# Full-array tiles and unread constant products in the block inversions of two attention stages

## The chip, the cores and the metric

The kernel runs on one core of one Trainium2 chip. The metric is the device time of the whole launch in microseconds, the median of several executions; lower is better. Everything is float32, except for five mask tables that are bfloat16.

## The reference, cut to what matters

The launch computes one network of four layers, each an attention block and a feed-forward block, on 8 batches of 512 rows of 128 columns. The change concerns two of the eight blocks: the first layer's attention (stage L0) and the third layer's (stage L2). Both are delta rules with 4 heads of 32 key columns. L0's reference has the step that matters, a triangular inverse of each chunk:

```python
A = jnp.where(tri, 0.0, -jnp.einsum('bhncd,bhned->bhnce', kb, k))
for i in range(1, chunk):
    upd = jnp.einsum('...k,...kj->...j', A[..., i, :], A[..., :, :i])
    A = A.at[..., i, :i].add(upd)
inv = A + jnp.eye(chunk, dtype=A.dtype)
u, w = inv @ v, inv @ kb
# per chunk, in order:
u_adj = ui - wi @ S
out_i = qi @ S + attn @ u_adj
S = S + jnp.swapaxes(ki, -1, -2) @ u_adj
```

L2 is the gated form of the same recurrence, stepwise in the reference. The kernel computes both in chunks of 128 rows: one 128x128 inverse for each chunk and head.

## The kernel before, in words

**Stages and lanes.** Eight stages run one after the other (`program`). Within a stage a unit is one batch of 512 rows (4 tiles). Two lanes work on two units at once; `weave` alternates their phases one by one, and every engine gets its instructions in that order. A lane has four PSUM banks `b[0..3]`. L0 and L2 have 8 units each, so 4 rounds of two units. A unit has four chunks, taken as two pairs.

**One pair of one unit**, in phases (`delta_phases`). The score products (L782) give the matrix `NT` and the masked attention `AT`. ScalarE copies `NT` out of PSUM in L0 (L1179); VectorE does in L2 (L2882). ScalarE then copies the four diagonal 32x32 blocks of `NT` into the tile `strict` (L856), laid out as 64x64 tiles with zeros beside the blocks. VectorE makes level 0 out of it: an add of the two halves, a mask product, a subtraction, a transposition (L885, 887, 889, 891).

**Levels 1 to 4** (`levels_pe`). Each has a left and a right phase. Left (L801): for each of the 8 matrices `m` two products of a 64x64 tile of `strict` with 32 columns of `x`. VectorE masks the result (L899). Right (L809): 32 products of 32x32 tiles with 16 columns. VectorE subtracts (L906) and transposes (L909), which gives the next `x`. The profile has two records for each float32 product, so a left phase is 32 records of L801 and a right phase 64 of L809.

**The joins**: `left_5`, `right_5`, `turn`, `left_6`, `right_6` (L817, 826, 834, 841, 848) put the 32-blocks together to 64 and then to 128, on tiles of 32x32 and 64x64.

**The chunks**: `carry`, `u`, `out`, one after the other over the chunks, on 128x128 tiles: in L0 L1089 and L1090, then L935, L1099 and L1101; in L2 L2663, L935, L2671 and L2675. Each carries the state `S` on.

**What else is in these stretches.** In L0 the first pair of every round has the products of the 64-tap filter between its phases: `next(between, None)` issues six products (12 records of L1243, 128x64 tiles with 16 columns) behind each phase. L2 has for each pair two products of `after` with 512 columns (L2651) ahead of the scores.

**Stage ends.** `meet_all` makes PE, ScalarE, VectorE and GpSimd wait on every semaphore that has a count, those of the DMAs too. `program` issues the load of the next stage's weights at the start of a stage; the stage function calls `meet_all` again after its first few instructions, so this wait includes the load just issued. `weights_landed` has a wait of its own on the current stage's weights.

**`held`** is one product and one ScalarE copy with bias (L1174) of L0, which stands among the key copies; PE waits for it ahead of the first scores.

Of the kernel before, what the change touches and what calls it, by code (L numbers as in the profile page):

```python
# [149 lines left out]

class Run:
# [22 lines left out]
    def meet(self, engine):  # L174

        for s in self.steps.values():
            if s.count:
                engine.wait_ge(s.sem, s.count)
# [240 lines left out]
def turn(pe, u, c, bank, blocks, name, rows=P):  # L419

    for t, block in enumerate(blocks):
        done = pe.transpose(bank[0:rows, t * P:(t + 1) * P], block, c("ident"))  # L422
    done.then_inc(*u.pe.step(name))

# [326 lines left out]

class Delta:
# [5 lines left out]
    def __init__(self, c, arena, dv, scaled):  # L758
# [6 lines left out]
        self.strict = arena.take(INVERTED, 2 * SMALL)  # L765
        self.strict_half = [self.strict[:, :, n * SMALL:(n + 1) * SMALL] for n in range(2)]
# [21 lines left out]
    def start_dve(self, dve, u):  # L788

        dve.memset(self.XT, 0.0).then_inc(*u.dve.step())  # L790
        dve.memset(self.strict, 0.0).then_inc(*u.dve.step("strict_cleared"))

    def levels_pe(self, pe, u, pair, between):
        b = u.banks
        for n in range(1, SMALL_LEVELS):
            pe.wait_ge(*u.dve.at(f"x{pair}_{n - 1}"))
            if n == 1:
                pe.wait_ge(*u.act.at(f"strict{pair}"))
            for m in range(INVERTED):
                for g in map(half_of, range(2)):  # L800
                    made = pe.matmul(b[2][g, m * SMALL:(m + 1) * SMALL], self.strict[g, m, :], self.x[g, m, :])  # L801
            made.then_inc(*u.pe.step(f"left{pair}_{n}"))
            next(between, None)
            yield f"left{pair}_{n}"
            pe.wait_ge(*u.dve.at(f"part{pair}_{n}"))
            half = SMALL // 2
            for m in range(INVERTED):
                for q in map(quarter, range(QUARTERS)):
                    made = pe.matmul(packed(b[3][q, m * half:(m + 1) * half], n), self.part[q, m, :],  # L809
                                     odd_blocks(self.xt[q, m, :], n))  # L810
            made.then_inc(*u.pe.step(f"right{pair}_{n}"))
            next(between, None)
            yield f"right{pair}_{n}"
# [6 lines left out]
        next(between, None)  # L820
        yield f"left{pair}_5"
# [7 lines left out]
        next(between, None)  # L829
        yield f"right{pair}_5"  # L830
# [12 lines left out]
        next(between, None)  # L843
        yield f"left{pair}_6"
# [8 lines left out]
    def strict_act(self, act, u, pair):  # L853

        for i in range(QUARTERS):
            act.copy(self.strict_half[i % 2][quarter(i)], self.NT8[quarter(i), :, quarter(i)]).then_inc(*u.act.step(f"strict{pair}"))  # L856
# [26 lines left out]
    def level0_dve(self, dve, u, pair):  # L883
        dve.wait_ge(*u.act.at(f"strict{pair}"))
        dve.tensor_tensor(self.part, *self.strict_half, ALU.add).then_inc(*u.dve.step())  # L885
        dve.wait_ge(*u.dve.last())
# [90 lines left out]
class L0AttnLane:  # L977
    def __init__(self, c, arena, vT, shortT, vearly, vrow):
# [3 lines left out]
        self.before = {name: arena.take(L0_ATTN_CONV - 1 + SEQ) for name in "qkv"}  # L982
        self.stat_rows = arena.take(TILES, HEADS, 32)
# [16 lines left out]
class L0Attn:  # L1000
    def __init__(self, run, w, arena, X):
# [7 lines left out]
                      for lane in range(LANES)]  # L1009
        self.units, self.filters, self.products = units_of(run, ["l0_attn"]), None, None  # L1010
# [29 lines left out]
    def pe(self, pe, u):  # L1040
        m, b, w, c = self.lanes[u.lane], u.banks, self.w, self.c
# [26 lines left out]
        turn(pe, u, c, b[2], tiles_of(m.qrow), "qT")  # L1068
        yield "keys"
# [3 lines left out]
        for pair in range(CHUNKS // 2):  # L1073
            if pair == 0:
                pe.wait_ge(*u.act.at("keyed"))
                pe.wait_ge(*u.act.at("held"))
            else:
                pe.wait_ge(*u.act.at("got1"))
                pe.wait_ge(*u.dve.at("state1"))
            yield from d.score_pe(pe, u, pair, m.kT, m.kbq)  # L1080
            yield from d.levels_pe(pe, u, pair, products)
            for j in range(2):
# [20 lines left out]
                made.then_inc(*u.pe.step(f"out{chunk}"))  # L1103
                yield f"out{chunk}"
# [33 lines left out]
    def act(self, act, u):  # L1138
# [27 lines left out]
        act.activation(m.rn, m.ss, ACT.Sqrt).then_inc(*u.act.step("norms"))  # L1166
        yield "norms"
# [5 lines left out]
        act.wait_ge(*u.pe.at("held"))  # L1173
        act.activation(m.zT, b[3][:, :], ACT.Identity, bias=w("fuse_b1")).then_inc(*u.act.step("held"))  # L1174
# [243 lines left out]
    def pool(self, pool, u):  # L1418
# [5 lines left out]
        for pair in range(CHUNKS // 2):  # L1424
            yield from delta_phases(pair)
# [1133 lines left out]
class L2AttnLane:  # L2559
    def __init__(self, c, arena):  # L2560
# [7 lines left out]
        self.conv = [all_heads(v) for v in (self.gt[:, 0], self.gt[:, 1], self.gtm[:, 0], self.gtm[:, 1])]  # L2568
        self.steps = [self.a, self.delta.T1[:, 0]]
# [10 lines left out]
class L2Attn:  # L2580
    def __init__(self, run, w, arena, X):
        self.run, self.c, self.w, self.X = run, run.c, w, X
        self.rate = arena.take(HEADS)
        self.lanes = [L2AttnLane(run.c, arena) for _ in range(LANES)]

# [11 lines left out]
    def pe(self, pe, u):  # L2597
        m, b, w, c = self.lanes[u.lane], u.banks, self.w, self.c
# [47 lines left out]
        for pair in range(CHUNKS // 2):  # L2646
            if pair > 0:
                pe.wait_ge(*u.dve.at("got1"))
            for j in range(2):
                pe.wait_ge(*u.dve.at(f"steps{pair}_{j}"))  # L2650
                pe.matmul(b[2 + j][:, :], c("after"), flat(m.steps[j])).then_inc(*u.pe.step(f"between{pair}_{j}"))  # L2651
            yield f"between{pair}"
# [3 lines left out]
            for j in range(2):  # L2656
# [19 lines left out]
                made.then_inc(*u.pe.step(f"out{chunk}"))  # L2676
                yield f"out{chunk}"
# [263 lines left out]
    def pool(self, pool, u):  # L2941
# [11 lines left out]
        for pair in range(CHUNKS // 2):  # L2953
            yield f"between{pair}"
            yield from delta_phases(pair)
# [918 lines left out]
```

## Time and profile before

| | |
|---|---|
| time, median of 3 runs | 5654.37 us (5648.27 to 5659.23) |
| the profiled execution's own time | 5665.99 us |
| its span, first to last instruction | 5664.6 us |
| PE busy in the span | 4062.2 us (72%) |
| VectorE, ScalarE, GpSimd busy | 3020.7, 1912.0, 818.4 us |
| mean granted TensorE clock | 0.76 of full speed |

The granted clock is the share of TensorE's full 2.4 GHz; it has two levels in this profile, 0.50 (1.2 GHz) and 1.00. A mean between them is a stretch with both. L0 runs from the start to about 1000 us, L2 from about 2844 to 3814 us.

### The profile page before, as it was taken

The numbers are of one execution on the slowest core, as the hardware profiler recorded it, in microseconds if no ns is written. First come the engines' busy times: TensorE is split into PE (matmuls) and PEld (weight loads), VectorE is DVE, ScalarE is ACT, GpSimd is POOL, SyncE is SP. The second block draws the span as 40 slices with busy tenths as digits, with TensorE's granted clock in tenths as the row PEclk, the third lists the DMA queues.
The fourth block names the chain that finished last, engine by engine and source line by source line (L and its number), as shares of the span: only waits on it lengthen the run. The fifth ranks groups of instructions, "written<-read, shape, count | busy, mean of one in ns | idle before, by whom it ended". The sixth has DMA issues, their size and how long they took to land.

```text
span 5664.6 us, 93833 instructions
## 1 busy us (share of the span) xinstructions
PE 4062.2 (72%) x39179; PEld 3146.2 (56%) x39228; DVE 3020.7 (53%) x8021; ACT 1912.0 (34%) x4196; POOL 818.4 (14%) x600
## 2 busy tenths in 40 slices
PE   6685967568878778773757768577777777776398
PEld 5574846446556555562646557464444555445377
DVE  4445364234554555547255665657666666665333
ACT  2234232123333333330232332325444455552122
POOL 0000000321011101101700000001222111110444
PEclk6555555677898898885756666668888998897599
DMA  9200000330000000001210000000000000000255
GB/s 266 54 2 1 2 1 1 105 113 1 1 1 1 1 1 1 1 1 37 31 41 1 1 1 2 1 2 1 1 1 1 1 1 1 1 1 17 72 164 141
DMA packets 140856, 152.26 MB, mean 27 GB/s; under 512 B 7809, under 2 KB 128003, under 8 KB 139793
## 3 DMA queue, kind: packets, MB, share of 16 engines
q1 hardware_dynamic: 119024, 128.21, 7.7%
q0 software_dynamic: 21408, 18.05, 1.9%
q8 instruction: 309, 5.06, 0.4%
q14 instruction: 115, 0.93, 0.1%
HBM read 87.38 MB, written 59.76 MB: 26 GB/s over the span
## 4 chain that ended last, share of the span: by engine, by line
PE 50%; DVE 29%; ACT 13%; issue 3%; POOL 3%; DMA 2%; SPq 0%; DVEq 0%; POOLq 0%; ACTq 0%
ACT work L3242 4%; PE banks_lane L801 4%; PE banks_lane L422 3%; PE banks_lane L3679 2%; PE banks_lane L1882 2%; PE banks_lane L809 2%; PE banks_lane L3128 2%; PE banks_lane L935 2%; PE banks_lane L3163 1%; ACT work L1976 1%; PE banks_lane L3108 1%; PE banks_lane L3150 1%; POOL room_l_ffn L569 1%; DVE work L2797 1%; DVE weights L3252 1%
## 5 line engine op out<-in xcount | busy, mean ns | idle before, releaser
L422 PE MATMUL banks_lane<-constants,work 128*128 128x128 f32 x968 | 194.4, 346 | 456.2 <-DVE work L408 209.2
L422 PEld LDWEIGHTS banks_lane<-constants,work 128*128 128x128 f32 x968 | 145.3, 178 | 524.9 <-DVE work L408 196.9
L422 PE MATMUL banks_lane<-constants,weights 128*128 128x128 f32 x596 | 126.2, 349 | 349.8 <-DVE weights L408 94.9
L402 POOL TENSOR_TENSOR weights<-weights,constants 128x4 f32<-128x4 f32 x76 | 78.6, 1034 | 1929.6 <-DVE weights L397 1929.6
L422 PEld LDWEIGHTS banks_lane<-constants,weights 128*128 128x128 f32 x596 | 89.3, 180 | 381.6 <-issue 175.0
L3242 ACT ACTIVATE work<-banks_lane,weights 128x192 f32<-128x192 f32 (+1 forms) x512 | 249.3, 505 | 132.5 <-DVE weights L3339 132.5
L402 POOL TENSOR_TENSOR work<-work,constants 128x4 f32<-128x4 f32 x76 | 77.5, 1019 | 1208.8 <-DVE work L397 1208.8
L3346 POOL TENSOR_TENSOR weights<-weights,constants 128x16 f32<-128x16 f32 x64 | 185.5, 2898 | 377.3 <-DVE weights L3254 377.3
L3335 DVE TENSOR_REDUCE weights<-banks_lane 128x2 f32<-128x384 f32 (+1 forms) x256 | 122.4, 520 | 140.2 <-PE banks_lane L3150 140.2
L2029 DVE TENSOR_REDUCE work<-banks_lane 128x2 f32<-128x512 f32 x256 | 158.8, 683 | 67.7 <-PE banks_lane L1896 67.2
L3163 PE MATMUL banks_lane<-constants,work 128*128 128x128 f32 x896 | 135.5, 297 | 80.7 <-DVE work L3327 42.2
L1976 ACT ACTIVATE work<-banks_lane 128x384 f32<-128x384 f32 (+1 forms) x256 | 118.5, 549 | 178.2 <-PE banks_lane L1917 110.0
L3163 PEld LDWEIGHTS banks_lane<-constants,work 128*128 128x128 f32 x896 | 108.1, 152 | 104.5 <-issue 57.0
L3679 PE MATMUL banks_lane<-weights,work 128*128 128x256 f32 x624 | 145.1, 386 | 14.5 <-DVE weights L3721 14.5
L3178 PE MATMUL banks_lane<-work 128*64 128x128 f32 x1792 | 128.1, 288 | 37.2 <-ACT work L3204 37.2
L656 POOL DMA_INDIRECT out<-weights,chunk_places x78 | 121.5, 1558 | 196.5 <-DVE chunk_places L648 130.3
L569 POOL DMA_INDIRECT room_l_ffn<-weights,indices x96 | 92.8, 966 | 362.1 <-DVE weights L392 324.7
L1882 PE MATMUL banks_lane<-weights,work 128*128 128x128 f32 x1024 | 136.7, 298 | 5.9 <-ACT work L1998 5.9
L1882 PEld LDWEIGHTS banks_lane<-weights,work 128*128 128x128 f32 x1024 | 132.7, 213 | 10.3 <-ACT work L1998 10.3
L801 PE MATMUL banks_lane<-work 64*64 64x32 f32 x2048 | 125.1, 292 | 16.5 <-DVE work L891 13.0
L3679 PEld LDWEIGHTS banks_lane<-weights,work 128*128 128x128 f32 x624 | 116.9, 192 | 34.0 <-DVE weights L3721 19.3
L3178 PEld LDWEIGHTS banks_lane<-work 128*64 128x64 f32 x1792 | 100.7, 142 | 62.2 <-ACT work L3204 49.6
(773 smaller groups left out, 10869.7 us busy)
## 6 DMA issues: line engine op xcount, KB each, us to landing
work<-experts_dram_l_ffn SPq DMA_DIRECT2D x39, 964.0 KB, 4.9
room_l_ffn<-work SPq DMA_DIRECT2D x30, 1188.0 KB, 14.7
work<-experts_dram_l_ffn SPq DMA_DIRECT2D x23, 512.0 KB, 3.6
weights<-weights_dram SPq DMA_DIRECT2D x1, 4833.5 KB, 14.3
work<-room_l_ffn SPq DMA_DIRECT2D x36, 132.0 KB, 4.0
weights<-weights_dram SPq DMA_DIRECT2D x1, 4112.0 KB, 13.1
weights<-bands_dram SPq DMA_DIRECT2D x1, 4096.0 KB, 13.1
weights<-room_l_ffn SPq DMA_DIRECT2D x26, 132.0 KB, 4.3
```

The source lines that it names most:

```text
L402: pool.tensor_tensor(n.rstd, n.rstd, c("neghalf", cols=(0, n.rstd.shape[1])), ALU.pow).then_inc(*u.pool.step(name))
L422: done = pe.transpose(bank[0:rows, t * P:(t + 1) * P], block, c("ident"))
L569: pool.indirect_dma_start(self.room, bass.IndirectOffsetOnAxis(ap=self.where[:, n, t:t + 1], axis=0), rows[n][:, t, :], None).then_inc(*se ...
L801: made = pe.matmul(b[2][g, m * SMALL:(m + 1) * SMALL], self.strict[g, m, :], self.x[g, m, :])
L1882: made = pe.matmul(b[1][:, cols_of(t)], m.ff[:, f, cols_of(t)], self.w(u, f"down{f}"), start=f == 0, stop=f == L1_ATTN_FF - 1)
L1976: act.activation(m.probs[:, hh, 0:blocks, :].rearrange("p b q -> p (b q)"), b[hh][:, 0:blocks * P], ACT.Exp, scale=L1_ATTN_SCALE).then_inc ...
L2029: dve.tensor_reduce(m.top[r][:, :, hh, L1_ATTN_HD], b[hh][:, :].rearrange("p (t c) -> p t c", t=2), AX, ALU.max, negate=True).then_inc(*u. ...
L3163: made = pe.transpose(u.banks[2 + side][:, cols_of(hh)], m.probs[n % 2][:, hh, side * P:(side + 1) * P], self.c("ident"))
L3178: made = pe.matmul(u.banks[2][rows, cols_of(j)], m.v[:, t - 1 + side, at:at + L2_FFN_HD], m.turned[n % 2][:, 4 * side + hh, :], start=side ...
L3242: act.activation(m.probs[n % 2][:, hh, L2_FFN_BACK + lo:2 * P], u.banks[side][:, j * span:(j + 1) * span], ACT.Exp, scale=m.q_factor[:, t, ...
L3346: pool.tensor_tensor(m.rn[:, t, :, :], m.rn[:, t, :, :], c("neghalf", cols=(0, 2 * L2_FFN_HEADS)).rearrange("p (n h) -> p n h", n=2), ALU. ...
L3679: made = pe.matmul(bank[:, g * CHUNK:(g + 1) * CHUNK], self.w(u, f"{name}{f}", cols=(g * P, (g + 1) * P)), m.z[:, f, :], start=f == 0, sto ...
```

## The change

The left phase takes `strict` as block-diagonal 128x128 tiles: 8 products of a 128x128 tile with 32 columns in the place of 16 of 64x64. The tiles are made by GpSimd, two products of `NT` with the constant `blocks32` for each pair (`blocks_pool`), written into buffers that are free then. ScalarE's four copies go into `part` directly, and VectorE's add of the halves and one memset go away. `keep_busy` issues products of two constant bfloat16 masks, a 128x128 tile with 512 columns, into a bank that nobody reads: one behind each half level and behind three of the join phases; in L0 2 (lane 0) or 8 (lane 1) behind the key transpositions; one behind a pair's first chunk, four behind the first pair's second chunk; in L2 four before and four behind the two products of each pair ahead of its scores. `held` moves ahead on ScalarE. `meet` leaves out the semaphores of the weights. In the cut diff below, the `keep_busy` line shown behind `left{pair}_{n}` also stands behind `right{pair}_{n}` and, with `FILL_JOIN`, behind `left{pair}_5`, `right{pair}_5` and `left{pair}_6`; L2's GpSimd program has the same two lines as L0's, with a wait on VectorE's `nt{pair}`. Fills by count: 264 in L0 (176 in levels and joins, 40 behind keys, 48 behind chunks) and 352 in L2 (176, 48, and 128 around the products ahead of the scores).

```diff
+WEIGHTS = [("DMA", f"weights{n}") for n in range(2)]
...
     def meet(self, engine):
-        for s in self.steps.values():
-            if s.count:
+        for key, s in self.steps.items():
+            if s.count and key not in WEIGHTS:
                 engine.wait_ge(s.sem, s.count)
...
+def keep_busy(pe, masks, place, n):
+
+    for _ in range(n):
+        pe.matmul(place, masks("ident"), masks("later"), start=True, stop=True)
...
+FILL_LEVEL, FILL_JOIN, FILL_CHUNK, FILL_PAIR, FILL_BETWEEN = 1, 1, 1, 4, 4
+FILL_KEYS = [2, 8]
...
-        self.strict = arena.take(INVERTED, 2 * SMALL)
-        self.strict_half = [self.strict[:, :, n * SMALL:(n + 1) * SMALL] for n in range(2)]
+        self.strict = None
...
         dve.memset(self.XT, 0.0).then_inc(*u.dve.step())
-        dve.memset(self.strict, 0.0).then_inc(*u.dve.step("strict_cleared"))
...
             if n == 1:
-                pe.wait_ge(*u.act.at(f"strict{pair}"))
+                pe.wait_ge(*u.pool.at(f"blocks{pair}"))
             for m in range(INVERTED):
-                for g in map(half_of, range(2)):
-                    made = pe.matmul(b[2][g, m * SMALL:(m + 1) * SMALL], self.strict[g, m, :], self.x[g, m, :])
+                made = pe.matmul(b[2][:, m * SMALL:(m + 1) * SMALL], self.strict[m // HEADS][:, m % HEADS, :], self.x[:, m, :])
             made.then_inc(*u.pe.step(f"left{pair}_{n}"))
             next(between, None)
+            keep_busy(pe, self.masks, b[0][:, :], FILL_LEVEL)
             yield f"left{pair}_{n}"
...
     def strict_act(self, act, u, pair):
         for i in range(QUARTERS):
-            act.copy(self.strict_half[i % 2][quarter(i)], self.NT8[quarter(i), :, quarter(i)]).then_inc(*u.act.step(f"strict{pair}"))
+            act.copy(self.part[quarter(i)], self.NT8[quarter(i), :, quarter(i)]).then_inc(*u.act.step(f"strict{pair}"))
+
+    def blocks_pool(self, pool, u, pair):
+
+        blocks = per_tile(self.c("blocks32"), HEADS)
+        for chunk in range(2):
+            pool.tensor_tensor(self.strict[chunk], self.NT[:, chunk], blocks, ALU.mult).then_inc(*u.pool.step(f"blocks{pair}"))
...
         dve.wait_ge(*u.act.at(f"strict{pair}"))
-        dve.tensor_tensor(self.part, *self.strict_half, ALU.add).then_inc(*u.dve.step())
-        dve.wait_ge(*u.dve.last())
         dve.tensor_tensor(self.part, self.part, per_tile(self.c("small0"), INVERTED), ALU.mult).then_inc(*u.dve.step())
...
         turn(pe, u, c, b[2], tiles_of(m.qrow), "qT")
+        pe.wait_ge(*u.act.at("held"))
+        keep_busy(pe, masks, b[3][:, :], FILL_KEYS[u.lane])
         yield "keys"
...
                 pe.wait_ge(*u.act.at("keyed"))
-                pe.wait_ge(*u.act.at("held"))
...
                 made.then_inc(*u.pe.step(f"out{chunk}"))
+                if chunk < CHUNKS - 1:
+                    keep_busy(pe, masks, b[0][:, :], FILL_PAIR if j else FILL_CHUNK)
                 yield f"out{chunk}"
@@ L0Attn.act, before yield "norms" @@
+        act.wait_ge(*u.pe.at("held"))
+        act.activation(m.zT, b[3][:, :], ACT.Identity, bias=w("fuse_b1")).then_inc(*u.act.step("held"))
@@ and before yield "keys" @@
-        act.wait_ge(*u.pe.at("held"))
-        act.activation(m.zT, b[3][:, :], ACT.Identity, bias=w("fuse_b1")).then_inc(*u.act.step("held"))
@@ L0Attn.pool @@
         for pair in range(CHUNKS // 2):
+            pool.wait_ge(*u.act.at(f"nt{pair}_{HEADS - 1}"))
+            m.delta.blocks_pool(pool, u, pair)
             yield from delta_phases(pair)
@@ L2Attn.pe @@
+            keep_busy(pe, masks, b[0][:, :], FILL_BETWEEN)
             for j in range(2):
                 pe.wait_ge(*u.dve.at(f"steps{pair}_{j}"))
                 pe.matmul(b[2 + j][:, :], c("after"), flat(m.steps[j])).then_inc(*u.pe.step(f"between{pair}_{j}"))
+            keep_busy(pe, masks, b[0][:, :], FILL_BETWEEN)
             yield f"between{pair}"
...
                 made.then_inc(*u.pe.step(f"out{chunk}"))
+                if chunk < CHUNKS - 1:
+                    keep_busy(pe, masks, b[1][:, :], FILL_PAIR if j else FILL_CHUNK)
```

## Rows read from the trace of the kernel before

**Rows 1.** The page: granted clock in 40 slices, in tenths.

```profile
PEclk6555555677898898885756666668888998897599
```

**Rows 2.** Windows: busy us of PE, PEld, DVE, ACT, POOL; clock; DMA.

```profile
318.00:331.00 13.00, 7.42 (x166) 5.40 (x164) 9.07 (x22) 9.06 (x23) 0.00 (x0) 1.00 0.01 2
340.00:349.00 9.00, 9.00 (x250) 8.65 (x248) 2.60 (x8) 0.00 (x0) 0.00 (x0) 0.50 0.01 4
377.00:396.00 19.00, 19.00 (x98) 18.54 (x96) 4.97 (x15) 2.19 (x7) 0.00 (x0) 0.50 0.00 1
2980.00:2987.00 7.00, 7.00 (x34) 6.34 (x32) 3.09 (x7) 0.37 (x1) 0.00 (x0) 0.50 0.00 0
2988.00:3000.00 12.00, 11.13 (x77) 9.00 (x76) 8.15 (x17) 2.31 (x5) 0.00 (x0) 1.00 0.00 0
```

**Rows 3.** The chain in L0, a first pair: start us, us, what.

```profile
340.44 1.85 PE banks_lane L801 x32
342.29 0.76 PE banks_lane L1243 x12
...
345.66 0.98 PE banks_lane L809 x64
...
349.14 1.85 PE banks_lane L801 x32
```

**Rows 4.** The chain in L0, second pair, the same columns.

```profile
408.62 3.63 PE banks_lane L801 x64
...
414.12 3.72 PE banks_lane L801 x63
```

**Rows 5.** Timeline of PE in L0 at clock 1.00: start, us, what.

```profile
325.67 1.17 PE L782 MATMUL banks_lane<-work 32*128 32x256 f32 x16 [2.50 <-ACT work L1174]
326.78 1.12 PE L801 MATMUL banks_lane<-weights,work 64*64 64x32 f32 x32
327.83 0.53 PE L1243 MATMUL banks_lane<-weights 128*64 128x16 f32 x12
329.68 0.73 PE L809 MATMUL banks_lane<-weights,work 32*32 32x16 f32 x64 [1.33 <-DVE work L899]
```

**Rows 6.** Timeline of PE, chunks of L0, then of L2.

```profile
380.36 1.91 PE L935 MATMUL banks_lane<-work,weights 128*128 128x32 f32 x8
...
385.07 1.90 PE L935 MATMUL banks_lane<-work 128*128 128x32 f32 x8
...
2987.17 1.10 PE L935 MATMUL banks_lane<-work 128*128 128x64 f32 x8
...
2990.44 1.10 PE L935 MATMUL banks_lane<-weights 128*128 128x64 f32 x8
```

**Rows 7.** Timeline of PE in L1: four bfloat16 mask products.

```profile
1341.19 1.10 PE L1891 MATMUL banks_lane<-masks 128*128 128x512 bf16 x4 [1.15 <-ACT work L1965]
```

**Rows 8.** The chain of the whole span: loads of weights.

```profile
1209.37 14.31 DMA weights<-weights_dram
...
2844.43 10.37 DMA weights<-weights_dram
```

**Rows 9.** Timeline: VectorE beside a GpSimd product, and alone.

```profile
1226.40 1.26 POOL L2080 TENSOR_TENSOR work<-work,weights 128x512 f32<-128x512 f32 x1
1226.47 2.05 DVE L408 TENSOR_SCALAR work<-work 128x128 f32<-128x128 f32 x4 [1.21 <-POOL work L402]
...
2857.63 1.12 DVE L408 TENSOR_SCALAR weights<-x_rows,weights 128x128 f32<-128x128 f32 x4 [1.25 <-POOL weights L402]
```

**Rows 10.** Timeline in L0: the copies and level 0 of one unit.

```profile
399.62 1.68 ACT L856 COPY work<-weights 32x256 f32<-32x256 f32 x4
...
401.34 0.42 DVE L885 TENSOR_TENSOR work<-work 128x256 f32<-128x256 f32 x1 [0.60 <-ACT work L856]
```

**Rows 11.** Timeline of PE in L2, ahead of a second pair's scores.

```profile
3003.73 3.18 PE L2651 MATMUL banks_lane<-work,constants 128*128 128x512 f32 x4 [3.83 <-DVE work L2873]
3007.60 2.11 PE L782 MATMUL banks_lane<-work 32*128 32x256 f32 x16 [0.69 <-ACT work L2760]
```

More of the change, by code:

```diff
@@ L812, in levels_pe @@
             next(between, None)
+            keep_busy(pe, self.masks, b[0][:, :], FILL_LEVEL)
             yield f"right{pair}_{n}"
@@ L820, in levels_pe @@
         next(between, None)
+        keep_busy(pe, self.masks, b[0][:, :], FILL_JOIN)
         yield f"left{pair}_5"
@@ L829, in levels_pe @@
         next(between, None)
+        keep_busy(pe, self.masks, b[0][:, :], FILL_JOIN)
         yield f"right{pair}_5"
@@ L843, in levels_pe @@
         next(between, None)
+        keep_busy(pe, self.masks, b[0][:, :], FILL_JOIN)
         yield f"left{pair}_6"
@@ L982, in __init__ @@
         self.before = {name: arena.take(L0_ATTN_CONV - 1 + SEQ) for name in "qkv"}
+        self.delta.strict = [self.before[name][:, L0_ATTN_CONV - 1:].rearrange("p (h n) -> p h n", n=P) for name in "qk"]
         self.stat_rows = arena.take(TILES, HEADS, 32)
@@ L1009, in __init__ @@
                       for lane in range(LANES)]
+        for m in self.lanes:
+            m.delta.masks = run.masks
         self.units, self.filters, self.products = units_of(run, ["l0_attn"]), None, None
@@ L1040, in pe @@
     def pe(self, pe, u):
-        m, b, w, c = self.lanes[u.lane], u.banks, self.w, self.c
+        m, b, w, c, masks = self.lanes[u.lane], u.banks, self.w, self.c, self.run.masks
         d = m.delta
@@ L2568, in __init__ @@
         self.conv = [all_heads(v) for v in (self.gt[:, 0], self.gt[:, 1], self.gtm[:, 0], self.gtm[:, 1])]
+        self.delta.strict = [self.gt[:, 0], self.gt[:, 1]]
         self.steps = [self.a, self.delta.T1[:, 0]]
@@ L2584, in __init__ @@
         self.lanes = [L2AttnLane(run.c, arena) for _ in range(LANES)]
+        for m in self.lanes:
+            m.delta.masks = run.masks
     def start_act(self, act, u):
@@ L2597, in pe @@
     def pe(self, pe, u):
-        m, b, w, c = self.lanes[u.lane], u.banks, self.w, self.c
+        m, b, w, c, masks = self.lanes[u.lane], u.banks, self.w, self.c, self.run.masks
         d = m.delta
@@ L2954, in pool @@
             yield f"between{pair}"
+            pool.wait_ge(*u.dve.at(f"nt{pair}"))
+            m.delta.blocks_pool(pool, u, pair)
             yield from delta_phases(pair)
```

## Prediction

> **What bounds the kernel now.** I read the page's slices first. PE is busy 72% of the span, but the clock row shows that this is often not work at full speed: the first slices (L0, 0 to 1000 us) and the middle ones (L2, from 2844 us) stand at 5 to 7 tenths, the stages between at 8 and 9 [rows 1]. Then the windows inside those two stages. In a first pair of L0, from 340 to 349 us, PE is busy 9.00 of 9.00 us at clock 0.50, 1.2 GHz; in the chunks from 377 to 396 us it is busy throughout, on 128x128 tiles, and still at 0.50. In L2 the clock goes from 0.50 to 1.00 at about 2987 us, behind some 7 us of full tiles with 64 and 256 columns, and stays up while such tiles go on [rows 2]. So being busy is not what raised it; streaming many columns through the full array is what the stretches with the high clock share, and the levels' small tiles and few columns are what those with the low clock share.
>
> Third, the chain. In the levels it runs on PE alone, piece behind piece: left phase 1.85 us, filter products 0.76, right phase 0.98, for two lanes; from one lane's left phase to its next is 349.14 - 340.44 = 8.70 us [rows 3], without filter products 414.12 - 408.62 = 5.50 us [rows 4]. VectorE and ScalarE are hidden behind the other lane. What PE issues, and at which clock, is therefore time one to one. There are 8 units by 2 pairs in each stage, two lanes at a time: 16 stretches in all, of 4 levels each, of which 4 (the first pairs of L0) have filter products.
>
> Last, the chain holds 14.31 and 10.37 us of waiting for weights [rows 8].
>
> **The change part by part, against the span of the profiled execution, if the clock holds in the levels.**
>
> *Left phase.* 16 records of a full tile with 32 columns take the place of 32 of 64x64. At half clock L935, the same shape, takes 1.91 us for 8 records [rows 6], so 16 take 3.5 to 3.8 (the tail of the first group lies under the second); I take 3.5, against 1.85 now. At full clock the trace has 64 columns, 1.10 us for 8 [rows 6]: 1.8 to 2.2 for 16, I take 1.9. So the new tile only breaks even at the double clock, and it costs 1.65 us more for each lane and level if the clock does not come.
>
> *Fills.* Four mask products of 512 columns take 1.10 us [rows 7], so one is 0.24 (without the shared tail) to 0.28; I take 0.24, and 0.48 at half clock. 616 of them are 148 us at full clock, 296 at half. In the levels nothing hides them, since PE is the chain. Ahead of the scores PE idles 3.83 us for VectorE in L2 [rows 11] and 2.50 us in L0 [rows 5]; the fills there cost nothing at full clock (8 are 1.9 us).
>
> *The rest of a level* at full clock: a right phase is 0.73 us with its tail, a group of filter products 0.53 [rows 5]; I take 0.55 and 0.40 from start to start. A level of both lanes is then 2 x (1.9 + 0.24 + 0.55 + 0.24) = 5.9 us, against 5.50: +0.4, over 12 stretches of 4 levels +17 us. With filter products 5.9 + 4 x 0.40 = 7.5, against 8.70: -1.2, over 16 levels -20 us. The levels themselves thus give nothing back; what is gained is what they let stay fast.
>
> *Joins.* Three fills for each lane, 1.4 us of both lanes at full clock and 2.9 at half, against small tiles that are halved where the clock is up; they are short chains through ScalarE. From -4 to +3 a stretch; I take -1: -16 us.
>
> *Chunks.* In L0 a step of one lane is 385.07 - 380.36 = 4.71 us at half clock; in L2 at full clock 2990.44 - 2987.17 = 3.27 [rows 6]. With a fill, three of four steps gain 1.2 us: 8 stretches, -29 us. L2's clock comes 7 us into its chunks [rows 2]; if it comes sooner, 0 to -3.5 us a stretch, I take -1.5: -12 us.
>
> *Scores of second pairs, and L2651.* A score phase is 2.11 us [rows 11], 1.17 at full clock [rows 5]. Two lanes in 4 stretches of L0: -8. In L2 about -2 for each of 8 stretches, L2651's 3.18 [rows 11] being nearly halved but waited for: -16. Together -24 us.
>
> *Held.* PE waits for it ahead of the second lane's scores [rows 5]; moved, it saves up to its 0.7 us four times: -3. Behind it on ScalarE stand the key copies, which wait for PE's transpositions anyway.
>
> *GpSimd.* Two products of 1.26 us [rows 9] stand where ScalarE's copies, 1.68 [rows 10], were what the first left phase waited for; VectorE loses one 0.42 us step of level 0 [rows 10]. GpSimd has nothing else queued in these phases. But beside a GpSimd product four VectorE instructions took 2.05 us that take 1.12 alone [rows 9], so level 0, with inputs from SBUF, may wait until GpSimd is done: 0.84 later, 0.42 shorter. At 0.4 us over 32 unit pairs +13 at most on the chain, half of it under the other lane; I take +8. The bounds are -13 (VectorE's step gained, nothing blocked) and 64 x 0.93 = +60.
>
> The Trainium skill, "SBUF — State Buffer", "Who interferes with whom", says that a VectorE instruction with two SBUF inputs and a GpSimd instruction reading SBUF block each other for a whole instruction. The trace agrees in kind, with 0.93 us lost beside one of 1.26; by the rule alone the bound would be 64 x 1.26 = 81 us in the place of 60.
>
> *Weights.* The two loads leave the chain and have a stage to land in: -24.7 us, sure.
>
> Sum: +17 - 20 - 16 - 29 - 12 - 24 - 3 + 8 - 25 = -104 us. The profiled execution's own time is 5666, so 5562; it lay 12 us above the median of the runs, so 5550.
>
> **The rivals.**
>
> *The clock falls in the levels (slower).* This is decided in one place. The new level has full tiles of 32 columns for 3.8 of 5.9 us, as the chunks of L0 that stayed at 0.50 have [rows 2], and fills of 512 columns for 1.0 us, which those lack. If fills and tiles are not enough, it falls behind the first level at full clock and nothing in the levels raises it again. A level is then 2 x (3.5 + 0.48 + 0.98 + 0.48) = 10.9 us against 5.50, with filter products 13.9 against 8.70: 5.3 more, for 3 levels of 16 stretches +254; joins +46; the chunks keep two thirds of their gain, -29; scores -20; the rest -20. Sum +231: 5885. It turns from gain to loss where about 20 of the 64 levels are at half clock. For it: the levels' average is not far from stretches that were slow. Against it: the clock is at 1.00 from 318 to 331 us, with PE busy only 7.42 of 13 us [rows 2], on full-tile transpositions, scores and one product of 512 columns: wide work with long gaps is enough. The fills also stand evenly, one behind each half level, and the filter products and joins are the only parts with less.
>
> *It falls in some stretches*, for instance in those with filter products, which dilute the fills: half way, +64: 5718.
>
> *GpSimd becomes what level 1 waits for, and blocks VectorE*, at the bound of +60 with the clock held: -52: 5602. For it rows 9; against it that only level 0 meets these products.
>
> *The Trainium skill*, "TensorE: Matmul & The Clock Gate", "Why this matters for your kernels", has it that keeping TensorE busy without long idle gaps gives the full clock. By that rule the clock would hold here, as in the forecast, but it would also have been up in the levels before, where 9.00 of 9.00 us busy stood at 0.50. The trace does not agree; I give the rule no more than the forecast has.
>
> **How the numbers follow.** Clock holds 0.58 (own range 5460 to 5610: joins and chunks wholly gained, or levels at the upper bounds of tile and fill); GpSimd blocks 0.07; falls in some stretches 0.14; falls in the levels 0.21. Same means within 0.2%, 11 us, about what a measurement of this kernel can tell from no change. Faster: 0.57 + 0.07 + 0.05 of the partial case = 0.69; same 0.04; slower 0.27. The range for 8 in 10 runs from 5440, below which only more gain than every part's bound would lead, to 5780, which takes in the partial case and leaves most of the last.
>
> **What would show it.** Right: windows in the levels of L0 and L2 at clock 0.9 to 1.0; left phases of about 1.9 us from start to start; 5.9 and 7.5 us a level; no piece of weights in the chain; chunk steps near 3.4 us in L0. Wrong: levels of 10 us or more at 0.50; idle time of PE ahead of the first left phase that GpSimd ends; level-0 instructions of VectorE of over 1 us; fills that delay the scores of the second lane.

## The result and the profile after

The changed kernel takes 5968.61 us (median of 4 runs, 5963.41 to 5985.8) against 5653.37 us before: ratio 1.0563, 95% interval 1.0539 to 1.0587. The recorded forecast was 5550 us, so it missed the sign. What came is the rival in which the clock falls in the levels, at +315 us by the medians and +297.5 by the spans (5962.1 and 5664.6), where the rival had +231 on the span. The ratio of fills2_entry4 below leaves out its slowest run, 5906.54 us, which is 1.8% above its fastest; its median is of all four.

The page of after, its first lines and the clock in 40 slices:

```profile
PE 4425.8 (74%) x37796; PEld 3367.0 (56%) x37796; DVE 3035.0 (51%) x7985; ACT 1913.2 (32%) x4196; POOL 900.0 (15%) x664
...
PEclk6555555577799888885766666666888898988599
```

PE has 364 us more to do and its clock is no higher: L0 is at 5 tenths from its second slice on, L2 at 6. Compare the clock row of before [rows 1]. Next, the windows (columns as in [rows 2]) in a first pair of L0, then in a first pair of L2:

```profile
361.00:366.00 5.00, 4.19 (x107) 3.47 (x106) 4.52 (x9) 2.84 (x8) 2.94 (x2) 1.00 0.01 3
366.00:380.00 14.00, 13.50 (x212) 12.19 (x213) 8.33 (x13) 0.00 (x0) 0.00 (x0) 0.52 0.01 2
380.00:412.00 32.00, 32.00 (x454) 28.77 (x453) 5.07 (x13) 0.81 (x2) 0.00 (x0) 0.50 0.01 2
...
3084.00:3089.00 5.00, 3.76 (x94) 2.79 (x86) 4.70 (x12) 1.61 (x4) 2.50 (x2) 1.00 0.00 0
3089.00:3093.00 4.00, 3.11 (x17) 3.12 (x18) 1.42 (x4) 0.00 (x0) 0.00 (x0) 0.69 0.02 4
3093.00:3110.00 17.00, 17.00 (x312) 14.78 (x312) 3.90 (x10) 0.00 (x0) 0.00 (x0) 0.50 0.01 2
```

The clock is 1.00 when level 1 starts, falls within it, and from there PE is busy without a gap at 0.50. In 15 of the 16 stretches it fell within level 1 (in three second pairs of L0 it had come up only in the first half us of it); in L0's first second pair, at 178.0 us, it stood at 0.50 throughout. Levels 2 to 4 are at 0.50 in all 16. The Trainium skill, "TensorE: Matmul & The Clock Gate", "Why this matters for your kernels", has it that an engine kept busy gets the full clock; 32.00 of 32.00 us busy at 0.50 is against it here, as [rows 2] were.

The timeline of PE in L0's first pair shows the fall and what a level costs behind it (start, us, line; in brackets idle time and its releaser; L811 is the left phase, L1268 the filter products, L432 the unread products, L820 the right phase):

```profile
360.94 1.97 PE L811 MATMUL banks_lane<-weights,work 128*128 128x32 f32 x16
362.84 0.53 PE L1268 MATMUL banks_lane<-weights 128*64 128x16 f32 x12
363.30 0.39 PE L432 MATMUL banks_lane<-masks 128*128 128x512 bf16 x1
364.48 0.73 PE L820 MATMUL banks_lane<-weights,work 32*32 32x16 f32 x64 [0.80 <-DVE work L918]
...
366.50 3.49 PE L811 MATMUL banks_lane<-work 128*128 128x32 f32 x16 [0.51 <-DVE work L910]
...
371.08 3.46 PE L811 MATMUL banks_lane<-weights,work 128*128 128x32 f32 x16
...
380.19 3.46 PE L811 MATMUL banks_lane<-work 128*128 128x32 f32 x16
```

From one lane's left phase to its next, 380.19 - 366.50 = 13.69 us, against 8.70 before [rows 3]; the rival had 13.9. The same in L2, without filter products:

```profile
3084.53 1.97 PE L811 MATMUL banks_lane<-weights,work 128*128 128x32 f32 x16
...
3087.87 0.73 PE L820 MATMUL banks_lane<-weights 32*32 32x16 f32 x64 [1.16 <-DVE weights L918]
...
3089.89 3.09 PE L811 MATMUL banks_lane<-work 128*128 128x32 f32 x16 [0.97 <-DVE work L910]
...
3093.20 3.46 PE L811 MATMUL banks_lane<-weights,work 128*128 128x32 f32 x16
...
3099.92 3.46 PE L811 MATMUL banks_lane<-work 128*128 128x32 f32 x16
...
3103.60 0.69 PE L811 MATMUL banks_lane<-weights,work 128*128 128x32 f32 x3
```

The other lane's left phases stand at 3093.20 and 3103.60: 10.40 us a level, against 5.50 before [rows 4]; the rival had 10.9. At half clock an unread product takes 0.40 us from its start to the next one's where a left phase follows and 0.54 where small tiles do. In these two the lane that comes first has its left phase of level 1 at clock 1.00, 1.97 us, about the 1.9 of the forecast; the other's takes 3.49 and 3.09.

Summed over the 16 stretches by the timelines of the two kernels (level 1's first left phase to `left_5`; `left_5` to the first L935, L954 in after; that to the last of the pair):

| us | levels | joins | chunks |
|---|---|---|---|
| before | 426 | 270 | 235 |
| after | 688 | 320 | 232 |

+262, +50 and -3 make +309; all else together gives back 12.

VectorE's timeline at the entry (L906 is level 0's mask product), and GpSimd's at the same time:

```profile
358.22 1.10 DVE L906 TENSOR_TENSOR work<-work,constants 128x256 f32<-128x256 f32 x1 [0.92 <-ACT work L871]
359.36 0.42 DVE L908 TENSOR_TENSOR weights<-constants,work 128x256 f32<-128x256 f32 x1
...
364.35 1.15 DVE L906 TENSOR_TENSOR work<-work,constants 128x256 f32<-128x256 f32 x1
```

```profile
356.55 2.50 POOL L877 TENSOR_TENSOR work<-weights,constants 128x512 f32<-128x512 f32 x2 [38.47 <-ACT weights L1204]
362.28 2.94 POOL L877 TENSOR_TENSOR work<-work,constants 128x512 f32<-128x512 f32 x2 [3.23 <-ACT work L1204]
```

Beside GpSimd's products L906 takes 1.10 and 1.15 us; L908, of the same size, 0.42 behind them, and each step of level 0 took 0.42 before [rows 10]. The add of 0.42 that went away is paid for with 0.7 on the step behind it. The Trainium skill, "SBUF — State Buffer", "Who interferes with whom", says that a VectorE instruction with two SBUF inputs and a GpSimd one that reads SBUF block each other; the trace agrees in kind, with 1.10 and 1.15 us in the place of 0.42.

### The profile page after: what moved, and what is told of

Same layout as the page of the kernel before. It is cut to its first block and busy times, and to the rows that moved or that the text cites. A ratio compares the mean times of both kernels' runs of the same rounds, so it can differ in the third digit from the quotient of the medians.

```text
span 5962.1 us, 91016 instructions
## 1 busy us (share of the span) xinstructions
PE 4425.8 (74%) x37796; PEld 3367.0 (56%) x37796; DVE 3035.0 (51%) x7985; ACT 1913.2 (32%) x4196; POOL 900.0 (15%) x664
## 5 line engine op out<-in xcount | busy, mean ns | idle before, releaser
L432 PE MATMUL banks_lane<-masks 128*128 128x512 bf16 x616 | 297.8, 533 | 3.5 <-ACT work L2787 3.5
L811 PEld LDWEIGHTS banks_lane<-work 128*128 128x128 f32 x1024 | 227.9, 328 | 21.8 <-DVE work L910 17.4
L811 PE MATMUL banks_lane<-work 128*128 128x32 f32 x1024 | 221.7, 392 | 12.1 <-DVE work L910 12.1
L811 PEld LDWEIGHTS banks_lane<-weights,work 128*128 128x128 f32 x1024 | 206.5, 300 | 13.8 <-DVE weights L910 5.5
L811 PE MATMUL banks_lane<-weights,work 128*128 128x32 f32 x1024 | 199.8, 366 | 2.6 <-DVE weights L910 2.6
L877 POOL TENSOR_TENSOR work<-weights,constants 128x512 f32<-128x512 f32 x32 | 40.0, 1272 | 1057.7 <-DVE weights L2916 535.4
L886 ACT COPY weights<-weights 32x256 f32<-32x256 f32 x32 | 12.9, 404 | 573.2 <-DVE weights L925 572.8
L918 DVE TENSOR_TENSOR work<-banks_lane,constants 128x256 f32<-128x256 f32 x96 | 40.8, 425 | 276.1 <-PE banks_lane L811 276.1
```

Of the source, the lines that this page charges most:

```text
L432: pe.matmul(place, masks("ident"), masks("later"), start=True, stop=True)
L811: made = pe.matmul(b[2][:, m * SMALL:(m + 1) * SMALL], self.strict[m // HEADS][:, m % HEADS, :], self.x[:, m, :])
```

## The experiments

Eleven kernels ran. Each ratio is against runs of the kernel before on the same chip; a difference of two ratios is turned into us with 5660. By their intervals such a difference is good to 25 to 40 us among the kernels with four runs and to about 10 among those with ten or more. "Fills" are the unread products of L432.

**1. no_level_fills**: the changed kernel, no fills in levels and joins.

```diff
-FILL_LEVEL, FILL_JOIN, FILL_CHUNK, FILL_PAIR, FILL_BETWEEN = 1, 1, 1, 4, 4
+FILL_LEVEL, FILL_JOIN, FILL_CHUNK, FILL_PAIR, FILL_BETWEEN = 0, 0, 1, 4, 4
```

> The changed kernel without the 352 fills in the levels and joins; tiles and all other fills as changed. Theory (the clock falls in level 1 and the fills are lost time at half clock): at half clock a fill adds 0.40 us behind a left phase and 0.54 behind small tiles, nothing hides them; some 300 of 352 stand at half clock: 352 x 0.45 = about -158 us, to 5810 +- 25, and the clock in levels 2 to 4 stays at 0.50. Rival (the fills do keep part of the levels at full clock and pay for themselves): 5968 or more.

5875.91 us, ratio 1.0359 (1.0327 to 1.0391): 0.0204 or 115 us under the changed kernel. The clock is at 0.50 in levels 2 to 4 here too. Levels 611, joins 268, chunks 249: the levels and joins are 129 us shorter, the chunks 17 longer, since L2's stand at 0.77 to 0.82 where six of the changed kernel's eight are at 1.00. A level at 0.50 is 8.9 us by PE's timeline in L2:

```profile
3048.94 3.62 PE L811 MATMUL banks_lane<-work 128*128 128x32 f32 x16
3052.37 3.60 PE L811 MATMUL banks_lane<-weights,work 128*128 128x32 f32 x16
3055.90 1.05 PE L820 MATMUL banks_lane<-work 32*32 32x16 f32 x64
...
3057.84 3.62 PE L811 MATMUL banks_lane<-work 128*128 128x32 f32 x16
```

3057.84 - 3048.94 = 8.90, so the four fills of a level add 10.4 - 8.9 = 1.5 us, not the 2 x 0.40 + 2 x 0.54 = 1.9 that they take themselves: with a fill behind it a left phase is 3.27 us from start to start (3096.47 - 3093.20 in the changed kernel's timeline), without one 3.43 and 3.53. That and the chunks are why 115 us went and not the 158 expected; the fills in levels and joins are still a third of the loss.

**2. old_tiles**: the changed kernel with the 64x64 tiles by ScalarE and VectorE's add, fills as in the change.

```diff
-                made = pe.matmul(b[2][:, m * SMALL:(m + 1) * SMALL], self.strict[m // HEADS][:, m % HEADS, :], self.x[:, m, :])
+                for g in map(half_of, range(2)):
+                    made = pe.matmul(b[2][g, m * SMALL:(m + 1) * SMALL], self.strict[g, m, :], self.x[g, m, :])
...
```

> The changed kernel with the left product on 64x64 tiles again, made by ScalarE as before; all fills stay. Theory: the tile costs 3.4 - 1.85 = 1.55 us for each lane and level at half clock, 128 of them, less where the clock was up, so -180 us, plus a little for the level-1 wait that GpSimd made: 5780 +- 25. The clock in the levels is 0.50 either way. Rival (the tiles carry what clock there is, and without them it is worse): above 5850.

5824.23 us, ratio 1.0261 (1.0225 to 1.0297): 0.0302 or 171 us under the changed kernel, for tile and GpSimd together. Levels 537, so 151 us shorter, joins and chunks as in the changed kernel; a level at 0.50 is 7.8 us (10.9 with filter products) in the place of 10.4 (13.7). Without GpSimd and without the full tile the clock fell in level 1 too, in 13 stretches, and in three second pairs of L0 it stood at 0.50 before; so neither is needed for the fall.

**3. entry4**: the changed kernel with four fills in level 1, one after it.

```diff
-            keep_busy(pe, self.masks, b[0][:, :], FILL_LEVEL)
+            keep_busy(pe, self.masks, b[0][:, :], 4 if n == 1 else FILL_LEVEL)
... (the same behind right)
```

> The changed kernel with 4 fills instead of 1 behind both halves of level 1 only. It asks where the clock is lost. Entry theory (level 1 has idle PE, 0.5 to 1.4 us at a time, behind VectorE's late level 0; once past it one fill a half level would hold): levels 2 to 4 at clock 1.00 in most stretches, a level 6 us instead of 10: more than 200 us faster than the change, below 5770. Fill theory (one fill a half level is too little anywhere): the clock falls in level 2, a few us later than now; 6 more fills for each of 32 lane stretches at 0.22 to 0.43 us: 5968 + 20 to 70, 5990 to 6040.

5915.67 us, ratio 1.0437 (1.04 to 1.0475): 71 us under the changed kernel and between the two forecasts. The timeline of PE in L2 (3055 us) shows the gaps shortened and the clock kept:

```profile
3057.87 0.73 PE L820 MATMUL banks_lane<-weights 32*32 32x16 f32 x64 [0.25 <-DVE weights L918]
...
3059.89 1.97 PE L811 MATMUL banks_lane<-work 128*128 128x32 f32 x16 [0.32 <-DVE work L910]
...
3067.08 1.87 PE L811 MATMUL banks_lane<-work 128*128 128x32 f32 x16
```

At 1.00 the levels behind level 1 take 6.4 and 5.8 us; 5.9 was forecast. In 12 of the 16 stretches the clock was kept through level 1; in four it fell there still, with idle times of 0.3 to 0.7 us. Only 5 of 16 stretches were still at 1.00 in level 3, and none came to the joins with it (joins 321, as in the changed kernel). The four first pairs of L0, with filter products, all fell in level 2, at a mean clock of 0.65 to 0.67 there, and took 13.7 us a level from then on. So what happens in level 1 decides whether the clock outlives it in most stretches, and one fill a half level does not keep it after that. Whether the idle time there or the little that is issued does it, this run does not separate, since the fills change both.

**4. fills3**: the changed kernel with FILL_LEVEL = 3.

> The changed kernel with 3 fills instead of 1 behind every half level. If three are enough, levels run at clock 1.00 and take 2 x (1.8 + 0.65 + 0.55 + 0.65) = 7.3 us instead of 10.1 (13.7 with filter products): about -130 us to -170 with what follows, 5800 to 5840, still slower than before the change. If they are not enough, 4 more fills of 0.43 us for each of 64 levels of two lanes ... 8 x 0.43 x 64 = +220: 6190.

5879.92 us, but from 5813.12 to 5957.23 in four runs; ratio 1.0365 (1.0298 to 1.0433). Windows of two stretches of the same code in one execution:

```profile
3342.00:3371.00 29.00, 28.00 (x617) 21.75 (x617) 12.12 (x31) 2.42 (x6) 2.50 (x2) 1.00 0.01 3
3514.00:3556.00 42.00, 40.80 (x621) 30.67 (x617) 12.67 (x32) 2.42 (x6) 2.50 (x2) 0.67 0.01 2
```

The same 617 products of four levels take 29 us where the clock stays and 42 where it falls in level 1 and comes back in level 3. It came back within the levels in 10 of the 16 stretches; in the changed kernel it never did. Two windows of another stretch, before and after the clock comes back in its level 3:

```profile
3007.00:3035.00 28.00, 27.57 (x345) 20.11 (x345) 6.83 (x16) 0.30 (x1) 1.17 (x1) 0.51 0.01 2
3035.00:3045.00 10.00, 10.00 (x251) 8.05 (x251) 3.05 (x8) 0.81 (x2) 0.00 (x0) 0.99 0.02 4
```

A level at 1.00 is 7.5 us, 9.6 with filter products: more than before at 0.50 (5.50 and 8.70).

**5. weights_only**: the kernel before, where `meet` leaves out the weights.

```diff
+WEIGHTS = [("DMA", f"weights{n}") for n in range(2)]
...
-        for s in self.steps.values():
-            if s.count:
+        for key, s in self.steps.items():
+            if s.count and key not in WEIGHTS:
```

> The kernel before with the weights' semaphores left out of meet, and nothing else. The two pieces of the chain, 14.31 and 10.37 us, go: -24.7 us, ratio 0.9956, if the load of the next weights disturbs nothing. Rival: the load that is now beside the stage's first work slows it, or something else stands at the same place, such as GpSimd or the rows' own load: -10 us or less.

5669.74 against 5676.41 us, ratio 0.9989 (0.9973 to 1.0004): 6 us where 24.7 were forecast. The chain at the start of L2 in this kernel:

```profile
2841.47 7.03 DMA x_rows<-spread
```

and VectorE's timeline at the start of L1 in the kernel before:

```profile
1216.80 0.91 DVE L1803 MEMSET work<- 128x1024 f32 x1 [0.28 <-DVE work L408]
...
1223.77 0.87 DVE L392 BATCH_NORM_STATS2 work<-work 128x6 f32<-128x128 f32 x4 [1.92 <-DMA weights<-weights_dram]
```

The wait for weights on the path was 1.92 us, not 14.31: under the load VectorE did two units' statistics and two sets of memsets that it has to do anyway. In L2, from x landed to the first statistics, it was 2854.88 - 2844.16 = 10.7 us before and 2852.67 - 2848.50 = 4.2 us here, 6.5 saved. The piece of the chain [rows 8] named what came last, not what it cost.

**6. old_tiles_bare**: as old_tiles, and no fills in levels and joins. Left of the change: weights, `held`, and 264 fills at keys, ahead of scores and in chunks.

> The changed kernel with the 64x64 tiles of before and no fills in levels and joins; what is left of the change is the weights' wait, held's place, and the 264 fills at keys, between, chunks and pair ends. Theory that all of the loss is the tile and the level and join fills: weights -25, held -3, the remaining fills about level (a chunk's fill costs 0.25 us a step in L0, the fills ahead of L2's scores stand in idle time, the clock comes a little sooner in L2's chunks): 5615 to 5640, faster than before. Rival, that the remaining fills are a loss of their own (264 x 0.25 to 0.43 = +66 to +110): 5690 or more.

5687.26 against 5676.41 us, ratio 1.0012 (0.9998 to 1.0025). Levels 426 and joins 272 are those of before; chunks 247 against 235. The fills in the chunks cost time, and the clock of the chunks is no higher: 0.50 in all of L0's, 0.76 to 0.84 in L2's, as before.

**7. fills2_entry4**: FILL_LEVEL = 2 with four in level 1.

> The changed kernel with 4 fills behind the half levels of level 1 and 2 behind the others. With 3 the clock held in some stretches and was lost in level 1 in others; with 4 in level 1 it was never lost there. If 2 are enough behind it: clock 1.00 in all 16 stretches, a level 6.4 us (8.0 with filter products), levels 460 us in sum instead of 688, joins and chunks as in the stretches of fills3 that stayed up: 5590 to 5620, faster than before, which would be the time of my forecast's kind. If 2 are not enough with filter products or in part of the stretches: 5700 to 5850.

5853.32 us (5802 to 5907), ratio 1.0278 (1.0231 to 1.0326). In L2 level 3 is at 1.00 in all 8 stretches, 6.7 us a level, and five kept the clock to the end. Three of L0's first pairs fell in level 2 and one in level 3 (15.4 us a level from then on), and of its second pairs three were at 0.50 when level 1 started and one fell in it. So four fills in level 1 do not always keep the clock there, as entry4's trace had shown. A held stretch of L2 takes 28.3 us in the levels, 12.4 in the joins and 10.9 to 11.6 in the chunks, 52 in all, against 23.7 + 16.1 + 13.4 = 53 before: holding the clock just pays for itself there.

**8. pool_only**: the kernel before, with GpSimd's two products for each pair into unread buffers, and PE's first left phase waiting for them.

```diff
+                pe.wait_ge(*u.pool.at(f"blocks{pair}"))
...
+            pool.tensor_tensor(self.unread[chunk], self.NT[:, chunk], blocks, ALU.mult).then_inc(*u.pool.step(f"blocks{pair}"))
...
```

> The kernel before with GpSimd's two products of NT with blocks32 for each pair added, written into the buffers of the change, where nobody reads them; PE's first left phase waits for them beside ScalarE's copies. Theory: VectorE's first level-0 instruction takes 1.10 us instead of 0.43 wherever a GpSimd product runs beside it, on the chain of each stretch once or twice: 16 to 32 times 0.3 to 0.7 us, +5 to +20 us. Rival (hidden by the other lane): within 0.1% of before. Second rival (it blocks far more of VectorE): +60.

5696.04 against 5676.41 us, ratio 1.0036 (1.0021 to 1.005): +20 us, 11 of them in the levels by the traces. VectorE's timeline has its first step of level 0 (L892 here) blocked, and the next not:

```profile
324.98 1.10 DVE L892 TENSOR_TENSOR work<-work 128x256 f32<-128x256 f32 x1 [0.98 <-ACT work L857]
326.11 0.42 DVE L894 TENSOR_TENSOR work<-work,constants 128x256 f32<-128x256 f32 x1
```

**9. full_hold**: the changed kernel with FILL_LEVEL = 5 and FILL_JOIN = 2.

> The changed kernel with 5 unread products behind each half level in the place of 1, and 2 in the place of 1 in the joins. It asks what a clock that holds in all 16 stretches is worth. Theory (holding costs more than it gives, since the full tiles at clock 1.00 only take what the 64x64 tiles took at 0.50): where three products behind a half level held the clock, a level took 7.5 us and 9.6 with filter products; two more behind each half level of both lanes are 8 x 0.23 = 1.8 us, so 9.3 and 11.4. Over 12 stretches of 4 levels and 4 with filter products that is 447 + 182 = 629 us against 426 before; joins about 258 against 270, chunks about 197 against 235. Sum +153 on the kernel before: 5780 to 5850, ratio 1.02 to 1.03, clock 0.50 in none of the levels. Rival (the recorded forecast's reason: what is gained is what the levels let stay fast): chunks, scores and joins give back most of it, 5700 or less. If the clock falls even here: over 6000.

5767.5 us (5746.39 to 5777.32), ratio 1.0205 (1.0187 to 1.0222), mean clock 0.842. Levels 2 and 3 are at 1.00 in 15 of 16 stretches (level 1 of L0's second pairs has a mean of 0.62 to 0.81), 9.2 us each without and 11.3 with filter products, by the timeline in L2:

```profile
3050.23 1.87 PE L811 MATMUL banks_lane<-work 128*128 128x32 f32 x16
...
3053.01 1.87 PE L811 MATMUL banks_lane<-weights,work 128*128 128x32 f32 x16
...
3059.48 0.75 PE L811 MATMUL banks_lane<-work 128*128 128x32 f32 x6
```

Levels 623, joins 233, chunks 173 us. So the held clock gives joins and chunks 37 + 62 = 99 us, and the levels take 197 more. The kernel with the highest clock in the levels is still 2% slower than the one at 0.50. It is also 0.0358, 203 us, faster than the changed kernel, with nearly three times its fills (1736 against 616).

**10. plain**: the kernel before with weights (as in weights_only, not shown again) and `held` alone.

```diff
         act.activation(m.rn, m.ss, ACT.Sqrt).then_inc(*u.act.step("norms"))
+        act.wait_ge(*u.pe.at("held"))
+        act.activation(m.zT, b[3][:, :], ACT.Identity, bias=w("fuse_b1")).then_inc(*u.act.step("held"))
         yield "norms"
...
-        act.wait_ge(*u.pe.at("held"))
-        act.activation(m.zT, b[3][:, :], ACT.Identity, bias=w("fuse_b1")).then_inc(*u.act.step("held"))
```

> The kernel before with two parts of the change alone: the stage ends leave out the weights, and held moves ahead on ScalarE. Tiles as before, no unread products. Theory: the weights are worth 6 us, as the run with that part alone showed, and held 0 to 3: 0.9975 to 0.9995 of the kernel before. Rival (the forecast's terms, 25 and 3): 0.995. This is also the candidate for a version that beats both kernels.

5640.71 against 5656.23 us, ratio 0.9975 (0.9963 to 0.9986): by the ratio 14 us faster than the kernel before, and so a version that beats both kernels, by a quarter of a per cent. By difference `held` would be 8 us of it, where 3 were forecast; the first left phase of L0's fourth round stands at 798 us, against 808 before and 806 in weights_only. The intervals of this run and of weights_only overlap, so the split is not sure. Against it old_tiles_bare is 0.0037, 21 us, slower: that is what the 264 fills outside levels and joins cost, 10 to 12 of it in the chunks.

**11. chunk_fills6**: plain, with six fills behind lane 0's first chunk in each pair of L0 (`keep_busy` as in the change).

```diff
                 made.then_inc(*u.pe.step(f"out{chunk}"))
+                if j == 0 and u.lane == 0:
+                    keep_busy(pe, self.run.masks, b[0][:, :], 6)
```

> The same kernel as the run with the weights and held alone, plus six unread products behind the first chunk of lane 0 in each pair of L0, 8 x 6 in all. It asks whether the chunks of L0 can be lifted from clock 0.50 alone. Forecast's reason (wide products raise the clock): behind six of them, 2.4 to 2.9 us, it goes to 1.00 and the three steps left take 3.3 us in the place of 4.7, -4.2: 8 x -1.5 = -12 us against that other run, 0.998 of it. Rival: it stays at 0.50 as in the chunks of the changed kernel, and the products cost 8 x 2.4 to 2.9 = +19 to +23 us, 1.0035 to 1.004 of it.

5637.22 us, ratio 0.9972 (0.996 to 0.9984): no different from plain. Both outcomes are in it, by windows (a first pair, then a second pair) and PE's timeline in that second pair (L157 the fills, L944 the values):

```profile
378.00:396.00 18.00, 17.78 (x87) 15.71 (x86) 2.63 (x9) 1.61 (x7) 0.00 (x0) 0.50 0.00 1
444.00:460.00 16.00, 12.66 (x85) 11.00 (x85) 6.61 (x20) 5.11 (x13) 0.00 (x0) 0.82 0.01 2
```

```profile
446.07 2.34 PE L157 MATMUL banks_lane<-masks 128*128 128x512 bf16 x5 [0.22 <-issue]
448.20 1.36 PE L944 MATMUL banks_lane<-work 128*128 128x32 f32 x8
...
451.06 1.06 PE L944 MATMUL banks_lane<-work,weights 128*128 128x32 f32 x8
...
453.61 1.06 PE L944 MATMUL banks_lane<-work 128*128 128x32 f32 x8
```

In three of the four second pairs the clock rose behind the fills, and a step took 2.9 and 2.6 us in the place of 4.7 [rows 6]: 13.3 to 13.8 us a pair against 16.0. In the other second pair and in the four first pairs it did not: 18.4. Why the same six products raise it in some and not in others stays open.

## Why the prediction was wrong

**The step that failed is the first: "if the clock holds in the levels", with 0.58.** It held in none of the 16 stretches. The reason given against the rival was that the clock stood at 1.00 from 318 to 331 us of L0 with PE only 7.42 of 13 us busy [rows 2], so "wide work with long gaps is enough". That window ends 0.7 us before the second lane's left phase of level 1, which is at half clock again in the timeline of the same kernel (1.92 us, against 1.12 at 326.78 in [rows 5]):

```profile
331.68 1.92 PE L801 MATMUL banks_lane<-work 64*64 64x32 f32 x32 [0.81 <-DVE work L891]
```

It was a clock about to fall, not one that such work was seen to keep. The other rounds of the same trace would have told: in the third and fourth the same transpositions and scores stand ahead of the levels, and there the clock was gone when level 1 began. By windows of the third:

```profile
559.00:567.00 8.00, 4.16 (x44) 3.22 (x44) 5.22 (x12) 5.06 (x12) 0.00 (x0) 0.91 0.00 0
567.00:572.00 5.00, 4.69 (x127) 4.17 (x120) 4.08 (x11) 2.85 (x8) 0.00 (x0) 0.52 0.01 3
```

In 13 of the 16 stretches of the kernel before, level 1 starts at 0.50. In plain, with the same work in the same place as in the forecast's window, it fell one step earlier, in the second lane's scores:

```profile
313.26 1.17 PE L785 MATMUL banks_lane<-work 32*128 32x256 f32 x16
...
318.98 1.82 PE L785 MATMUL banks_lane<-work 32*128 32x256 f32 x16 [1.93 <-ACT work L1177]
```

What is shown: the fall comes in level 1, in which PE idles 0.3 to 1.4 us at a time behind VectorE; four fills there move it to level 2 or later in 12 of 16 stretches (entry4); with one fill a half level it then always falls before the joins; with two (and four in level 1) level 3 is at 1.00 in all of L2 and the clock falls beside filter products; with five it stays nearly everywhere. Whether it is the idle time or the little that is issued that costs the clock stays open. Of these places the forecast named the filter products and the joins ("the only parts with less") and gave them too little weight; the idle times of level 1, of which [rows 5] show one of 1.33 us, it did not name.

**Point by point.**
- Left phase: 3.46 us at half clock (3.5 forecast, from [rows 6]) and 1.70 to 1.80 from start to start at full (1.9). Right.
- A fill: 0.24 and 0.48 forecast; 0.40 to 0.54 at half clock, and from 5.8, 6.7, 7.5 and 9.2 us a level with one, two, three and five fills, 0.2 each at full. Right.
- A level held: 5.9 forecast, 5.8 measured, against 5.50 before. That the levels give nothing back was right; it also means that there was little to win.
- A level fallen: 10.9 and 13.9 in the rival; 10.4 and 13.7 measured. Levels +254 against +262, joins +46 against +50. That nothing in the levels raises the clock again was right for the changed kernel, and not with three fills (fills3).
- Chunks: -41 forecast, of which the rival kept -29; measured -3, and +12 in old_tiles_bare. The clock of L0's chunks stayed at 0.50: a step is 445.78 - 440.82 = 4.96 us by the timeline below against 4.71 before. L2's chunks did gain (12.0 and 11.4 us a pair against 13.5 and 13.2, 13 us in all); L0's first pairs lost 2.1 each and its second 0.5, 10 us in all. For L0 it is the failed step once more, not a size: the clock did not come out of the levels, and the fills in the chunks did not raise it.

```profile
440.82 1.75 PE L954 MATMUL banks_lane<-work 128*128 128x32 f32 x8
...
445.37 0.61 PE L432 MATMUL banks_lane<-masks 128*128 128x512 bf16 x1
445.78 1.54 PE L954 MATMUL banks_lane<-work,weights 128*128 128x32 f32 x7
```

- Weights: -25 called sure; -6 measured, and that interval reaches zero. Mis-sized for want of a look at what else ran under the load.
- `held`: -3 against about -8. GpSimd: +8 against +20 in pool_only, which keeps ScalarE's copies and VectorE's add, within its bounds; the block on level 0 was told with the right size (0.93 us from [rows 9]; 0.7 measured).
- The rival's +231 was worked out against the spans, where +297.5 was measured: 66 us short, of them chunks 26, weights 19, levels and joins 12. The other 9 no run here takes apart. Against the medians' +315 it is 18 more, since the profiled execution lay 12 us above the median before and 5 below it after.

Step by step from plain to the changed kernel, by ratios: 264 fills outside levels and joins +21 us, fills in levels and joins +141 (old_tiles against old_tiles_bare), the tile with GpSimd +171. Taken off first, the fills in levels and joins are 115 (no_level_fills). That is 26 us less, no more than the intervals allow for, but the traces have it too: in the levels the same fills add 110 us with the old tiles (537 against 426) and 77 with the full ones (688 against 611).

## What to carry to other kernels

A stretch at the high clock tells what keeps it only if it goes on long after what came before it; read the rows at its end first. Work issued for the clock has to be priced at the low clock too, and the held state compared with the old one: here the new tile and one fill at full clock take as long (5.8 us) as the old tile at half (5.5), so even success gave next to nothing, and failure cost 5 us a level. A wait in the chain is worth what would be late next, not its length.

## What the hardware showed unexpectedly

The same instructions in the same execution took 29 or 42 us, by whether the clock fell (fills3), and kernels near that edge scattered by 104 and 144 us from run to run (fills2_entry4 and fills3), where 22 runs of the kernel before on one chip stayed within 29. Full 128x128 tiles with 32 columns at 32.00 of 32.00 us busy and small tiles, a product of 512 columns behind each half level, stayed at 0.50. Nearly three times the unread products (full_hold against after) made the kernel 203 us faster.
